# Spiral scan: four strided history entries a ring, summed by TensorE, and every second final update on ScalarE and GpSimd

## The reference, cut to what matters

```python
def step(g, inp):
    ci, ni, nm, nc = inp
    local = g[:, ci, :]
    nb = g[:, ni, :]
    neigh = (nb * nm[None, :, None]).sum(axis=1) / nc
    u = jnp.concatenate([local, neigh], axis=-1)
    y_sc = jnp.tanh(u @ w1 + b1) @ w2 + b2
    g = g.at[:, ci, :].set(local + y_sc[:, None] * w_y[None, :])
    return (g, None)
```

## Time and profile before

| | us |
|---|---|
| median of 3 runs | 4940.8 (4936.7 to 4956.19) |
| profiled execution | 4956.47 |
| its span in the trace | 4954.6 |
| busy in the span: TensorE, VectorE, ScalarE, GpSimd | 4515.9, 4011.1, 2520.8, 3487.0 |

### The profile page before, as it was taken

How to read it: one execution, slowest core, us unless ns; L and a number is a source line. 1 busy time by engine, 2 the same in 40 slices (tenths; PEclk the granted TensorE clock), 3 DMA queues, 4 the chain that set the end, 5 groups by cost and what they waited for, 6 DMA issues and landing times.

```text
span 4954.6 us, 62164 instructions
## 1 busy us (share of the span) xinstructions
PE 4515.9 (91%) x19323; PEld 3290.4 (66%) x19323; DVE 4011.1 (81%) x6107; ACT 2520.8 (51%) x4454; POOL 3487.0 (70%) x2478
## 2 busy tenths in 40 slices
PE   3999999999999999999999999888888888888875
PEld 2788888888788888888878887644444444444432
DVE  5888888988886888888888887288888888877753
ACT  3566666666566566656656665333444443333321
POOL 3888888888887888888888888566666655554321
PEclk7999999999999999999999999999999999999976
DMA  3344444444444444444444443499999988876530
GB/s 92 116 130 139 132 138 134 135 137 134 132 137 135 132 139 131 138 129 140 131 137 132 139 127 126 168 310 298 294 317 288 285 273 259 242 226 188 166 107 27
DMA packets 395139, 835.31 MB, mean 169 GB/s; under 512 B 76864, under 2 KB 178496, under 8 KB 394688
## 3 DMA queue, kind: packets, MB, share of 16 engines
q1 hardware_dynamic: 251408, 420.08, 31.3%
q0 software_dynamic: 143408, 411.26, 22.2%
HBM read 419.95 MB, written 425.85 MB: 171 GB/s over the span
## 4 chain that ended last, share of the span: by engine, by line
PE 70%; ACT 10%; DVE 9%; issue 7%; DMA 2%; POOL 1%; SPq 0%; DVEq 0%; POOLq 0%; ACTq 0%
PE psum L846 12%; PE psum L848 12%; PE psum L847 12%; PE psum L830 12%; PE psum L859 10%; DVE psum L704 4%; ACT relu_rows L531 4%; PE psum L819 3%; PE psum L868 3%; PE psum L878 2%; PE psum L880 2%; DMA out<-dw_rows 2%; ACT u_hi L554 2%; PE psum L879 2%; ACT psum L549 2%
## 5 line engine op out<-in xcount | busy, mean ns | idle before, releaser
L629 DVE SCALAR_TENSOR_TENSOR dw_rows<-relu_rows,taps,dw_rows 128x1792 f32<-128x1792 f32 x872 | 1805.2, 2081 | 25.4 <-ACT dw_rows L520 20.3
L445 POOL DMA_INDIRECT s_x<-xo,wave_idx x784 | 1365.5, 1742 | 315.3 <-issue 215.9
L464 POOL DMA_INDIRECT out<-dw_rows x897 | 891.9, 994 | 860.4 <-DVE dw_rows L712 623.8
L846 PE MATMUL psum<-w_hi,u_hi 128*128 128x512 f32 x3136 | 1385.1, 442 | 0.0
L451 POOL DMA_INDIRECT s_pre<-eo,wave_idx x784 | 1207.8, 1541 | 247.5 <-issue 229.5
L848 PE MATMUL psum<-w_hi,u_lo 128*128 128x512 f32 x3136 | 1233.3, 393 | 0.0
L847 PE MATMUL psum<-w_lo,u_hi 128*128 128x512 f32 x3136 | 1226.4, 391 | 0.0
L859 PE MATMUL psum<-dw_rows,ident 128*128 128x512 f32 x1794 | 978.7, 628 | 161.5 <-DVE near L704 155.3
L485 ACT ACTIVATE eo<-psum 128x512 f32<-128x512 f32 x784 | 468.1, 597 | 1222.9 <-PE psum L848 1123.9
L549 ACT ACTIVATE psum<-psum 128x512 f32<-128x512 f32 x897 | 522.1, 582 | 914.2 <-PE psum L868 914.2
L830 PE MATMUL psum<-pw,dw_rows 128*128 128x256 f32 x3136 | 820.4, 385 | 63.7 <-ACT psum L540 59.4
(11 more groups left out here) (88 smaller groups left out, 3919.1 us busy)
## 6 DMA issues: line engine op xcount, KB each, us to landing
dw_rows<-s_pre SPq DMA_DIRECT2D x615, 256.0 KB, 3.9
x_tok<-x SPq DMA_DIRECT2D x112, 896.0 KB, 6.8
dw_rows<-s_x SPq DMA_DIRECT2D x615, 128.0 KB
dw_rows<-s_pre SPq DMA_DIRECT2D x169, 192.0 KB, 3.6
dw_rows<-s_x SPq DMA_DIRECT2D x169, 96.0 KB
out<-dw_rows POOLq DMA_INDIRECT x897
s_x<-xo,wave_idx POOLq DMA_INDIRECT x784, 3.3
s_pre<-eo,wave_idx POOLq DMA_INDIRECT x784, 3.4
```

The source lines that it names most:

```text
L445: pool.indirect_dma_start(s_x, bass.IndirectOffsetOnAxis(wave_idx[:, n:n + 1], 0), xo[:, n % XO_SLOTS, :], None, bounds_check=TILES * P - ...
L464: pool.indirect_dma_start(out_rows, bass.IndirectOffsetOnAxis(store_idx[:, c:c + 1], 0), o_t[:, c % OUT_SLOTS, :], None, bounds_check=OUT_ ...
L629: dve.scalar_tensor_tensor(out=dst, in0=pair_rows(relu_rows, k + ky - 1, c, 2 * kx * NB), scalar=taps[:, c, 3 * ky + kx:3 * ky + kx + 1], ...
L846: pe.matmul(bank, hi, w_hi[:, k, :], start=k == 0, stop=False)
```

## The change

It has four parts, all in the scan.

1. Of each ring's history only the entries at distance 1, 3, 5 and 7 have coefficients other than zero, so WIN is 4 in place of 7, read with a stride of 2.
2. The product of these (now 3 x (n + 1) x 4 elements for n groups, the three copies included) is the operand of turn itself: the columns are laid out as three blocks of 8 rings by 4 terms, and sel, which picks the row of v_sel, takes all four terms of a ring (part_i % B // WIN == i), so that add_sums' product adds them up. The reduction L739 and the tiles inner are gone. own uses only the first of the four places. turn's shifted product starts WIN columns later and not one.
3. finish on VectorE remains for even tiles, in the iteration of the next tile. For odd tiles ScalarE forms the product wy_row * y (product, into one of two slots, behind the tanh two tiles later), and GpSimd adds x_t to it ahead of its store. The semaphore out_ready is split in two.
4. VectorE's order for a tile is dot(c), neighbours, finish(c - 1) if c is odd, sum_rows. sum_rows has moved to min(last + 2, use - 1) in all cases.

```diff
-WIN = 7
+WIN = 4
...
-        sel[:, i] = ((part_i < 3 * B) & (part_i % B == i)) | (part_i == 3 * B) | (part_i == 3 * B + 1)
+        sel[:, i] = ((part_i < 3 * B) & (part_i % B // WIN == i)) | (part_i == 3 * B) | (part_i == 3 * B + 1)
...
             for c in range(TILES):
-                pool.wait_ge(out_ready, c + 1)
+                if c % 2:
+                    pool.wait_ge(prod_ready, c // 2 + 1)
+                    pool.wait_ge(xt_in[c % XT_SLOTS], 16 * (c // XT_SLOTS + 1))
+                    if c >= OUT_SLOTS:
+                        pool.wait_ge(tile_out[c % OUT_SLOTS], 16 * (c // OUT_SLOTS))
+                    pool.tensor_tensor(o_t[:, c % OUT_SLOTS, :], prod[:, c // 2 % PROD_SLOTS, :],
+                                       x_t[:, c % XT_SLOTS, :], ALU.add).then_inc(out_ready[1], 1)
+                pool.wait_ge(out_ready[c % 2], c // 2 + 1)
                 pool.indirect_dma_start(out_rows, bass.IndirectOffsetOnAxis(store_idx[:, c:c + 1], 0),
...
+            def product(c):
+
+                level, g = SEQ[c]
+                act.wait_ge(y_ready, c + 1)
+                if c // 2 >= PROD_SLOTS:
+                    act.wait_ge(out_ready[1], c // 2 - PROD_SLOTS + 1)
+                act.activation(prod[:, c // 2 % PROD_SLOTS, :], wy_row, ACT.Copy,
+                               scale=hist[:, g, PAD + level:PAD + level + 1]).then_inc(prod_ready, 1)
...
                 act.activation(psum[:, c % BANKS, :], psum[:, c % BANKS, :], ACT.Tanh).then_inc(th_ready, 1)
+                if c > 1 and c % 2:
+                    product(c - 2)
...
                 dve.wait_ge(y_ready, c + 1)
-                dve.tensor_tensor(win[part][:, 0:n + 1, :], hist[:, g0:g1 + 1, level + 1:level + 1 + WIN],
-                                  coef_in_sb[:, at_in:at_in + (n + 1) * WIN].rearrange("p (g w) -> p g w", w=WIN),
-                                  ALU.mult).then_inc(win_ready, 1)
...
+                dve.tensor_tensor(terms(win[part], 0, n + 1, WIN),
+                                  thrice(hist[:, g0:g1 + 1, level + 1:level + 8:2], n + 1, WIN),
+                                  thrice(coef_in_sb[:, at_in:at_in + (n + 1) * WIN].rearrange(
+                                      "p (g w) -> p g w", w=WIN), n + 1, WIN), ALU.mult).then_inc(win_ready, 1)
...
-                dve.wait_ge(win_ready, S_COUNT[part, level])
-                dve.tensor_reduce(blocks(inner[part], 0, n + 1),
-                                  win[part][:, 0:n + 1, :].rearrange("p (o g) w -> p o g w", o=1).broadcast_to(
-                                      [P, 3, n + 1, WIN]), axis=AX.X, op=ALU.add).then_inc(in_ready, 1)
...
             for c in range(TILES):
                 dot(c)
-                if c:
+                for part, level in NEIGHBOURS_AT.get(c, ()):
+                    neighbours(part, level, c)
+                if c % 2:
                     finish(c - 1)
                 for part, level in SUM_ROWS_AT.get(c, ()):
                     sum_rows(part, level)
-                for part, level in NEIGHBOURS_AT.get(c, ()):
-                    neighbours(part, level, c)
-                for part, level in SUM_ROWS_NOW.get(c, ()):
-                    sum_rows(part, level)
+            assert TILES % 2
             finish(TILES - 1)
...
-        late = min(last + 1, use - 1)
         high.setdefault(min(last + 2, use - 1), []).append((part, level))
-        (rows_now if late == last else rows_late).setdefault(late, []).append((part, level))
-    return neighbours, turns, high, rows_late, rows_now, count, done
...
+        rows.setdefault(min(last + 2, use - 1), []).append((part, level))
```

More of the change, by code:

```diff
@@ L53 @@
 X_BEHIND = 4
+PROD_SLOTS = 2
 V_ROWS = 4
@@ L179, in shape_tables @@
                 else:
-                    assert r2 == r - 1 and 1 <= d <= WIN and g2 - g == (q == 0)
-                    coef_in[rows, AT_IN[part, level] + (g2 - g0) * WIN + WIN - d] = 1.0 / len(near)
+                    assert r2 == r - 1 and d in (1, 3, 5, 7) and g2 - g == (q == 0)
+                    coef_in[rows, AT_IN[part, level] + (g2 - g0) * WIN + (7 - d) // 2] = 1.0 / len(near)
     part_i = np.arange(P)
@@ L280, in build @@
         wrap_sb = in_relu.take(2 * (LEVELS // 8)).rearrange("p (k n) -> p k n", k=2)
[L282 to L287, removed]
+        win_near = Region(near[:, :, :, :].rearrange("p a b c -> p (a b c)"), N_SLOTS * CK * NROW)
+        hist = win_near.take((GROUPS + 1) * HIST).rearrange("p (g n) -> p g n", g=GROUPS + 1)
+        shift_sb = win_near.take(2 * P).rearrange("p (k n) -> p k n", k=2)
+        own = [win_near.take(3 * B) for _ in range(2)]
+        win = [win_near.take(3 * B + WIN) for _ in range(2)]
         in_dw = Region(dw_rows[:, :, :, :].rearrange("p a b c -> p (a b c)"), D_SLOTS * CK * DROW)
@@ L291, in build @@
         x_t = in_dw.take(XT_SLOTS * C).rearrange("p (k n) -> p k n", k=XT_SLOTS)
+        prod = in_dw.take(PROD_SLOTS * C).rearrange("p (k n) -> p k n", k=PROD_SLOTS)
         o_t = in_dw.take(OUT_SLOTS * C).rearrange("p (k n) -> p k n", k=OUT_SLOTS)
@@ L343, in build @@
         win_ready = sem("win_ready")
-        in_ready = sem("in_ready")
         own_ready = sem("own_ready")
@@ L348, in build @@
         s_ready = sem("s_ready")
-        out_ready = sem("out_ready")
+        prod_ready = sem("prod_ready")
+        out_ready = [sem("out_ready_dve"), sem("out_ready_pool")]
         tile_out = [sem(f"tile_out{i}") for i in range(OUT_SLOTS)]
@@ L458, in _ @@
                 pool.memset(own[part], 0.0)
-                last = pool.memset(inner[part], 0.0)
+                last = pool.memset(win[part], 0.0)
             last.then_inc(cleared, 1)
@@ L554, in _ @@
                     act.activation(s_rows[0:96, part, :], psum[0:96, BANKS + part, 0:P], ACT.Copy).then_inc(hi_row, 1)
+            product(TILES - 2)
         @block.vector
@@ L713, in finish, with thrice, terms @@
                                          in1=x_t[:, c % XT_SLOTS, :], op0=ALU.mult,
[L714 to L722, removed]
+                                         op1=ALU.add).then_inc(out_ready[0], 1)
+            own_ops, win_ops = 0, 0
+            def thrice(ap, n, w):
+                return ap.rearrange("p (o g) w -> p o g w", o=1).broadcast_to([P, 3, n, w])
+            def terms(buf, i, n, w):
+                blocks = buf[:, 0:3 * B].rearrange("p (k g w) -> p k g w", k=3, w=WIN)
+                return blocks[:, :, i:i + n, 0:w]
             def neighbours(part, level, c):
-                nonlocal own_ops, in_ops
+                nonlocal own_ops, win_ops
                 g0, g1 = groups_of(part, level + 1)
@@ L871, in turn @@
             def turn(part, level):
-                a, b = own[part], inner[part]
+                a, b = own[part], win[part]
                 t = psum[0:96, BANKS + part, 0:P]
-                own_n, in_n = SUMS_DONE[part, level]
+                own_n, wwin_n = SUMS_DONE[part, level]
                 pe.wait_ge(own_ready, own_n)
-                pe.wait_ge(in_ready, in_n)
+                pe.wait_ge(win_ready, wwin_n)
                 pe.matmul(t, a, ident[:, :], start=True, stop=False)
                 pe.matmul(t, b[:, 0:3 * B], shift_sb[:, 0, :], start=False, stop=False)
-                pe.matmul(t, b[:, 1:3 * B + 1], shift_sb[:, 1, :], start=False, stop=True).then_inc(s_turned, 1)
+                pe.matmul(t, b[:, WIN:3 * B + WIN], shift_sb[:, 1, :], start=False, stop=True).then_inc(s_turned, 1)
             pe.wait_ge(s_ready, 1)
@@ L898, in sums_order @@
 def sums_order():
-    neighbours, turns, high, rows_late, rows_now, count, done = {}, {}, {}, {}, {}, {}, {}
-    own_n = in_n = n = 0
+    neighbours, turns, high, rows, count, done = {}, {}, {}, {}, {}, {}
+    own_n = win_n = n = 0
     order = []
```

45 lines of the change are left out of this document (23 added, 22 removed).

## The result

The changed kernel takes 5188.1 us (5187.3 to 5193.6, 4 runs), against 4946.4 for the kernel before in the same session (4936.7 to 4956.2, 4 runs): a ratio of 1.049, interval 1.0468 to 1.0511. The forecast was slower, but 42 us slower and not 242; the time lies far outside the range.

A forecast was written before the change was run, and what follows sets the result against it. Hand-over loops, different in each stage, were taken to bound the kernel, no engine being full. Stage terms 2 + 9 + 10 + 5 + 19 + 11 - 14 gave 42 us more, a median of 4983 us, range 4925 to 5040.

The forecast's parts named there:

- the pair on GpSimd: Stages 0 and 1: two scatters and an add per two tiles take 3.25 us; 2 and 9 us more.
- The add, taken at 0.57: GpSimd's 128x256 add for odd tiles, priced at twice a 0.28 us select, between 0.28 and 1.13.
- The hand-over, taken at 0.1: Allowance of 0.1 us for hand-overs in GpSimd's two-tile cycle, beside 0.30 before each scatter.
- An add over 0.7: Sign that the prediction is wrong: GpSimd's add takes over 0.7 us (or under 0.35).
- The other signs: GpSimd's gap only issue in stages 0 and 1; L731 0.85 to 0.90 behind dot; L868 waits longer in stages 2 to 5.
- six double steps and two turn steps for 14 tiles: TensorE's cycle in stage 0, steps of 2.9 and 1.78 us, said to give 10.6 us a level.
- stalls that before has over its loop: Stages 0 and 1: 0.15 and 0.35 us a level added to GpSimd's time, giving 11.6 and 10.1.
- the rival that was given 0.15: GpSimd's add and VectorE's finish or products block each other: 97 us more, 5038 us; chance 0.15.
- The order: VectorE's new order holds back sums in stages 2 to 5: 10, 5, 19 and 11 us more.
- TensorE's loop: Stages 0 and 1: chain between add_sums operations, alone giving 10.6 and 9.4 us a level.
- ScalarE's product: 448 products of 128x256 on ScalarE: priced at nothing, up to 0.38 us an odd tile without cover.
- Stage 6: One tile a level: earlier neighbours and no reduction save 0.44 us on each of 32 levels, 14 us less.

The follow-up runs named there:

- e5: Changed kernel with GpSimd's order altered: the even tile's scatter stands between the odd tile's add and its own scatter; 5182.4 us, ratio 1.0438.
- e2: Kernel before plus only the offload (odd tiles' product on ScalarE, add on GpSimd), with old sums and old order; 5149.9 us, ratio 1.0393.
- e10: Changed kernel with eight slots of o_t in place of four, nothing else; 5170.7 us, ratio 1.0436.
- e7: Changed kernel with a GpSimd copy of the product in place of its add, x left out of odd tiles; 5084.8 us, ratio 1.0238.
- e4: Changed kernel with the old order on VectorE (finish, sum_rows at last + 1, neighbours), new sums and offload kept; 5130.7 us, ratio 1.0358.
- e9: Changed kernel with the even tile's scatter between add and its own scatter, and eight slots of o_t in place of four; 5034.2 us, ratio 1.0161.
- e6: Changed kernel without GpSimd's add: ScalarE writes odd tiles' product straight into the stored slot, x left out there; 4966.8 us, ratio 1.0014.
- e3: Kernel before with only the new sums (strided window, no reduction), old order and no offload; 4936.2 us, ratio 0.9969.
- e1: Changed kernel without the offload: all final updates on VectorE, new sums and new order kept; 5032.9 us, ratio 1.0158.
- e11: New sums, no offload, against the kernel before: VectorE runs dot, sum_rows at last + 2, finish, neighbours; one-tile stage has neighbours before finish; 4845.2 us, ratio 0.9777.
- e8: New sums, no offload, against the kernel before: sum_rows at last + 2 in stage 0, old order in 1 to 5, neighbours first in 6; 4919.1 us, ratio 0.9911.

## Why the prediction was wrong in size

**The step that failed** is the pair on GpSimd, "a pair costs 2 x 1.29 + 0.67 = 3.25". Its mechanism was right and two of its terms were too small. The add, taken at 0.57, is 0.72 alone and 0.77 in stage 0. The hand-over, taken at 0.1 on top of the scatter's own 0.30, is 0.49 on top of it: the scatter reads what the add wrote and waits for GpSimd's own semaphore, and that wait isn't hidden, as e5 shows by filling it. That makes a pair of 3.85, so 13.5, 11.5 and 9.6 us a level in stages 0 to 2, which is 62 + 56 + 36 = 154 us over the kernel before. Measured were 187, forecast 21: the two terms are 133 of the 166 that were missing there, and e2 and e10 run these stages within 0.2 us a level of the changed kernel. So GpSimd's pair bounds stage 2 as well, which the forecast left to VectorE's order. The range around the add reached up to 1.13 in the text, but the case that it made was never worked out to a time: 3.8 a pair is 13.3 us a level in stage 0, and the high end of the range should have been at least there. The 0.1 had no row of its own, and no range. An add over 0.7 was one of the prediction's own signs of being wrong, and it came: the mean is 0.76. The other signs read as forecast: GpSimd has next to no gap ahead of an add in stages 0 and 1, L755 stands 0.90 behind dot, and TensorE waits longer for sum_rows in stages 2 to 5.

Two smaller terms don't come out of the rows. The prediction's own steps for stage 0 (six double steps and two turn steps for 14 tiles) give 10.5 and not 10.6. And the "stalls that before has over its loop" are 0.9 and 0.4 by its own levels (11.53 - 10.6 and 9.81 - 9.4), where it adds 0.15 and 0.35; no row or run shows the 0.15. Neither decides anything beside the pair. The length of stage 5 that it lists, 183, is 186 by its sum.

**The second miss** is the rival that was given 0.15: add and finish block each other. L734 with 1.00 in the timeline above shows it, and the whole trace does: all 146 finishes that take over 0.6 us overlap an add, and of the 290 under 0.5 only 6 do. The other way round, all 58 adds over 0.85 us overlap a finish or a product. The exclusion rule of the Trainium skill ("SBUF — State Buffer", Who interferes with whom) agrees with these overlaps. It is no alternative to the forecast; it comes on top. Stages 3, 4 and 5 measured 8.2, 7.2 and 6.0 where the order alone gives 7.5, 6.8 and 5.7 or 5.8, and with a copy in the add's place they measured 7.7, 6.9 and 5.9. Between e7 and the changed kernel lie 15 + 9 + 4 us, of the 40 that were missing in these stages (75 measured, 35 forecast). In stage 3 the pair itself, 3.85 for two tiles, would be a rival, as e2, e4 and e10 run that stage at its rate. But in e5 and e9 the pair is 3.2 and GpSimd stands idle for some 0.88 us ahead of each add there, and stages 3, 4 and 5 still take 8.3 or 8.1, 7.2 and 6.0. In stage 5 of the changed kernel, one odd tile:

```profile
4900.34 0.76 DVE L726 CUSTOM_DVE_ANT_0 psum<-psum,dw_rows,b_col 128x512 f32<-128x512 f32 x1 [1.21 <-ACT psum L568]
...
4900.80 0.72 POOL L470 TENSOR_TENSOR dw_rows<-dw_rows 128x256 f32<-128x256 f32 x1 [2.11 <-ACT dw_rows L562]
4901.12 0.08 DVE L726 DVE_READ_ACCUMULATOR2_ANT near<- 128x1 f32 x1
4901.24 0.32 DVE L755 TENSOR_TENSOR near<-near,relu_rows 128x24 f32<-128x24 f32 x1
...
4901.56 0.47 DVE L734 SCALAR_TENSOR_TENSOR dw_rows<-dw_rows,near 128x256 f32<-128x256 f32 x1
...
4902.06 0.29 DVE L788 TENSOR_TENSOR u_hi<-psum,u_hi 32x128 fp32r<-32x128 f32 x1
...
4902.40 0.50 PE L887 MATMUL psum<-u_hi 128*128 128x512 f32 x1 [1.20 <-DVE u_hi L788]
```

The add runs from 4900.80 to 4901.52. The first product of neighbours, L755, asked for at 4901.24, takes 0.32 and not 0.18. Here the price is small, since the add stands over a short instruction; with finish under it, in stage 3, finish averages 0.70, and 0.49 in e7 (groups of instructions in that stage, first the changed kernel, then e7):

```profile
L734 DVE SCALAR_TENSOR_TENSOR dw_rows<-dw_rows,near 128x256 f32<-128x256 f32 x64 | 44.8, 700 | 0.4 <-DMA out<-dw_rows 0.4
...
L734 DVE SCALAR_TENSOR_TENSOR dw_rows<-dw_rows,near 128x256 f32<-128x256 f32 x64 | 31.2, 487 | 0.0
```

**Right, point by point.** *The order* costs what was worked out: dot to L755 is 0.90 in this timeline (0.85 was taken), and with nothing from GpSimd in the way (e6) stages 2 to 5 took 8.9, 7.7, 6.9 and 5.8 against 8.8, 7.5, 6.8 and 5.7 by the sum. e3 against e1 puts it at 97 us where all tiles have their finish on VectorE. *TensorE's loop* of 9.4 in stage 1 and 10.6 in stage 0 is the floor that e1, e6 and e11 ran near (9.6 to 9.7, and 11.0 to 11.1, in e1 with DMA at 0.94 and 313 GB/s, close to the ceiling that was named; which of the two holds stage 0 there was not tried). *ScalarE's product* cost little (e6). *Stage 6* was to give 14 and gave 17. *The reduction* was worth next to nothing outside loops: 0.997 (e3). *The order and the offload don't add up*: from the scan's start in the profiled executions, the order costs 92 us where all finishes are on VectorE (e1 against e3) and 60 with the offload (changed against e4). The difference lies in stages 3 to 5, where half of the finishes no longer stand between neighbours and sum_rows and where, in stage 3, the old order was already at the pair's rate.

**Open** is how finish and add share the reads in detail, by operand count or by length, since e7 changed both. By the three stages above it is worth 28 us; in stages 0 to 2 it is also in the add, 0.77 where it takes 0.72 alone, which on 288 pairs is an estimate of some 15 us more. Why GpSimd needs 0.80 us between its add and the scatter that waits for it is open as well. The clock of 0.95 in stages 0 to 2 wasn't separated either.

## What to carry to other kernels

Before an instruction is given to GpSimd, write out its whole cycle: the instruction, the gap behind it if the next one reads its result, and the work that is already there. Here it was 0.77 + 0.80 on top of 2.3, on an engine that looked 60% busy. In a queue that runs in order, ask what stands between an operation and the one that a later tile waits for: the same operations cost 97 us in one order (e1 against e3), and another gave 61 to 74 (e11 against e8). And when a bound is removed, look for the buffer that was sized for it: the pair without its gap gave 36 us of the scan with four slots (e5) and 145 with eight (e9 against e10).

## What the runs showed of the hardware that was not expected

- A wait of GpSimd for its own result is dear: 0.80 us from the end of an add or a copy to the start of a scatter that waits for it, in every stage of the changed kernel and of e7; 0.16 us in e5, where the scatter behind the add waits for something that has long been there.
- A 128x256 add on GpSimd takes 0.72 us alone, a copy 0.40 to 0.43; an eighth of the Trainium skill's 2048-element add gave an estimate of 0.56 ("GPSIMD Engine Reference", Elementwise — side-by-side cycle accounting). That the difference is a part that doesn't shrink with the size is a guess: no second size was run.
- A VectorE finish of 0.48 us takes up to 1.28 where it overlaps GpSimd's add (4771.92, stage 4); a product of 0.16 up to 0.79 when it starts while the add is only next in GpSimd's queue (in stage 0 one ran from 3519.54 to 3520.33, beside a scatter that ended at 3520.19, and the add began at 3520.21). Before the change, beside scatters alone, the longest of these products took 0.22; what holds it was not tried.
